# Attention on one Trainium2 core: the next group's loads put ahead of the spreading of reciprocals, and divided otherwise over four gaps

## The reference

```
qkv = (h @ Wqkv.T + bqkv).reshape(B, N, num_heads, hd, 3)
energy = einsum('bhqd,bhkd->bhqk', q, k)
att = softmax(energy, axis=-1) / D ** 0.5
out = einsum('bhqk,bhkd->bhqd', att, v)
out = out.reshape(B, N, D) @ Wp.T + bp
h1 = out + hidden
y = _sln(h1, ...) + h1
```

## Time and profile before

| | |
|---|---|
| median of 3 runs | 1860.88 us (1857.96 to 1861.51) |
| the profiled execution's own time | 1862.02 us |
| its span, first to last instruction | 1859.5 us |
| PE busy | 1810.8 us (97%) |
| POOL busy | 1217.2 us (65%) |
| DVE, ACT busy | 1256.5 us (68%), 835.2 us (45%) |
| attention | from about 900 us to 1769 us of the span |

### The profile page before, as it was taken

How to read it: one execution, slowest core, us unless ns; L and a number is a source line. 1 busy time by engine, 2 the same in 40 slices (tenths; PEclk the granted TensorE clock), 3 DMA queues, 4 the chain that set the end, 5 groups by cost and what they waited for, 6 DMA issues and landing times. The chain is left out here.

```text
span 1859.5 us, 26833 instructions
## 1 busy us (share of the span) xinstructions
PE 1810.8 (97%) x9510; PEld 1210.0 (65%) x9510; DVE 1256.5 (68%) x1986; ACT 835.2 (45%) x1545; POOL 1217.2 (65%) x679
## 2 busy tenths in 40 slices
PE   8899999999999999999999999999999999999997
PEld 4588888888888788888545554555555455544476
DVE  4665655655655565556777777787777777777487
ACT  3223122222223222221466666666666666666465
POOL 2675465465464243332588888888888898889665
PEclk9999999999999999999999999999999999999899
DMA  7310110110103667594877877787778777765796
GB/s 268 121 35 23 57 35 23 56 34 23 58 1 124 204 213 239 180 295 179 198 155 178 187 174 179 175 187 176 179 180 182 179 180 176 183 152 126 224 385 252
DMA packets 135382, 287.21 MB, mean 154 GB/s; under 512 B 23985, under 2 KB 41521, under 8 KB 127201
## 3 DMA queue, kind: packets, MB, share of 16 engines
q1 hardware_dynamic: 102996, 200.10, 35.5%
q0 software_dynamic: 9264, 66.11, 17.5%
q10 hardware_dynamic: 23008, 19.54, 3.3%
HBM read 134.68 MB, written 84.19 MB: 118 GB/s over the span
## 5 line engine op out<-in xcount | busy, mean ns | idle before, releaser
L1634 DVE TENSOR_REDUCE at_mrow<-banks 128x1 f32<-128x512 f32 x976 | 593.6, 680 | 166.0 <-PE banks L1480 165.8
L1730 POOL TENSOR_TENSOR at_sums<-at_probs 128x2048 f32<-128x2048 f32 x127 | 598.5, 4713 | 92.3 <-DMA at_sums<-at_sums 81.4
L1614 ACT ACTIVATE at_probs<-banks 128x512 f32<-128x512 f32 x1024 | 519.2, 623 | 182.1 <-PE banks L1498 176.7
L1480 PE MATMUL banks<-early_ks,early_qs 96*128 96x512 f32 x976 | 406.9, 417 | 8.8 <-DVE at_mrow L1634 5.0
L1498 PE MATMUL banks<-early_qs,early_ks 98*128 98x512 f32 x1024 | 408.9, 418 | 1.9 <-ACT at_probs L1614 1.9
L1480 PEld LDWEIGHTS banks<-early_ks,early_qs 96*128 96x128 f32 x976 | 184.8, 189 | 141.5 <-DVE at_mrow L1634 88.4
L1498 PEld LDWEIGHTS banks<-early_qs,early_ks 98*128 98x128 f32 x1024 | 193.6, 190 | 106.4 <-ACT at_probs L1614 82.5
L1510 PE MATMUL banks<-at_probs,at_v 128*32 128x512 f32 x2048 | 251.1, 608 | 0.8 <-DMA at_v<-v_scratch 0.8
L66 PE MATMUL banks<-l_nt,l_weights 128*128 128x512 f32 x768 | 177.9, 392 | 5.9 <-DVEq L1208 4.8
L662 ACT ACTIVATE l_gt<-banks,mod 128x512 f32<-128x512 f32 x60 | 45.1, 777 | 299.0 <-PE banks L528 261.4
L66 PE MATMUL banks<-l_ht,l_weights 128*128 128x512 f32 x768 | 177.4, 390 | 1.9 <-issue 1.9
(11 more groups left out here) (147 smaller groups left out, 2160.6 us busy)
## 6 DMA issues: line engine op xcount, KB each, us to landing
at_sums<-at_sums POOLq DMA_DIRECT2D x63, 1024.0 KB, 8.1
qk_scratch<-qk_out SPq DMA_DIRECT2D x64, 512.0 KB, 6.3
early_ks<-qk_scratch SPq DMA_DIRECT2D x48, 512.0 KB, 4.9
early_qs<-qk_scratch SPq DMA_DIRECT2D x96, 256.0 KB, 5.7
attn_scratch<-at_out SPq DMA_DIRECT2D x32, 512.0 KB, 7.5
o_a<-attn_scratch SPq DMA_DIRECT2D x32, 512.0 KB, 13.1
chunk_in<-x SPq DMA_DIRECT2D x8, 1024.0 KB, 5.3
v_scratch<-qk_v ACTq DMA_DIRECT2D x32, 256.0 KB, 2.6
```

Of the source, the lines that this page charges most:

```text
L1480: pe.matmul(em[n % 3][:], qs[0:96, slot, half, j, c * P:(c + 1) * P], ks[0:96, slot, j, keys * CH:(keys + 1) * CH], start=True, stop=True) ...
L1614: nc.scalar.activation(probs[:, i % 4, j, :], et[n % 3][:], ACT.Exp).then_inc(exp_done, 1)
L1634: nc.vector.tensor_reduce(mrow[:, half, keys, u:u + 1], em[n % 3][:], AX.X, ALU.max).then_inc(max_done, 1)
L1730: nc.gpsimd.tensor_tensor(into, probs[:, a], probs[:, a + 1], ALU.add).then_inc(pair_ready, 1)
```

## The change

Three things change in what SP does in attention; no other engine's order changes.

First, `load_part` divides the ten pieces otherwise: in units of 256 KB the four gaps had 5, 2, 5 and 2 and now have 3, 4, 3 and 4. By pieces they were 3, 1, 5, 1 and are 2, 3, 2, 3. Second, `widen_rden` is cut in two: `keep_rden` stores the reciprocals, `widen_rden` waits for that and loads them back. Third, gap 1 and gap 3 now stand between the two halves, so their loads are issued ahead of the loads of reciprocals. In the last group the second and the fourth gap of `load_projection` move in the same way.

```diff
-                    load_stack_keys(sp, sh, ks, g, slot, (0, 1))
+                    load_stack_keys(sp, sh, ks, g, slot, (0,))
                     load_stack_queries(sp, sh, qs, g, slot, 0, (0,))
                 if part == 1:
+                    load_stack_keys(sp, sh, ks, g, slot, (1,))
+                    load_stack_queries(sp, sh, qs, g, slot, 0, (1, 2))
+                if part == 2:
                     load_stack_keys(sp, sh, ks, g, slot, (2,))
-                if part == 2:
-                    load_stack_queries(sp, sh, qs, g, slot, 0, (1, 2))
-                    load_stack_queries(sp, sh, qs, g, slot, 1)
+                    load_stack_queries(sp, sh, qs, g, slot, 1, (0,))
                 if part == 3:
+                    load_stack_queries(sp, sh, qs, g, slot, 1, (1, 2))
                     load_v(g, slot)
...
-            def widen_rden(g, half):
+            def keep_rden(g, half):
...
                 sp.dma_start(sh.rden_d[half].rearrange("j (r c) -> (j r) c", c=DW), rden_c[:, half]).then_inc(rden_stored[half], 16)
+
+            def widen_rden(g, half):
+
+                first = isinstance(g, int) and g == 0
                 sp.wait_ge(rden_stored[half], 16 * (g + 1))
...
                 place_neg(g, slot, 1)
                 if not first:
+                    keep_rden(g - 1, 1)
+                fetch(1)
+                if not first:
                     widen_rden(g - 1, 1)
-                fetch(1)
                 fetch(2)
                 spread_den(g, 0)
...
                     place_neg(g + 1, (slot + 1) % RING, 0)
+                keep_rden(g, 0)
+                fetch(3)
                 widen_rden(g, 0)
-                fetch(3)
```

## The result

The changed kernel takes 1881.1 us (median of 6, 1876.9 to 1884.3) against 1860.2 us (median of 6, 1858.0 to 1861.5): a ratio of 1.0117, 95% interval 1.0105 to 1.0129. It is slower by 1.2%, as forecast in sign and within the range; the forecast was 1872.5, so 9 us of the 21 were missing in it. The profiled execution spans 1879.6 us, 20.1 more than that of before.

A forecast was written before the change was run, and what follows sets the result against it. POOL's chain of quad landings, adds and multiplications, not PE, was taken to set the pace. Groups +8 us and the end +3 made +11 on the profiled 1862.0: 1873, given as 1872.5 us; 8-in-10 range 1853 to 1901.

The forecast's parts named there:

- SP's DMAs are served in the order of issue: Reciprocals land behind the loads of gaps 1 and 3: 8.1 and 7.5 us after the quad.
- rival 5: Queues take turns, so quad 1 slows the loads still ahead of the reciprocals: 5.4 us more a group, 1942 us; 7%.
- `multiply` moves by 2.5 and 2.0 us: On POOL, in half 1 and half 0, the multiplication starts that much later, waiting for reciprocals behind the gap's loads.
- from `multiply` to the next quad's issue it takes 11.38 us: On POOL, the least time for this stretch; it was 12.06 us, of which 0.68 is air that the delay uses up.
- quads 0 and 2 get faster, to 7.6 us: With 512 KB less just ahead in gaps 0 and 2, landing to add included; before 9.1 and 9.5, bounds 7.2 and 8.8.
- Rival 4: Quads don't get faster (8.8 us), since their slowness is the store's doing: 1903 us; 13%.
- a group takes 53.6 us: Sum of both halves, 27.1 and 26.5 us, against 53.09 before: +0.5 us a group.
- POOL's chain: Landing, add, DMA issue, `multiply`, add, add, DMA issue, landing; said to set the halves' pace, 26.73 and 26.36 us before.
- rival 1: Emptier queue wins: reciprocals within 6.5 us, quads in 7.2, PE's own work bounds, maxima wait comes back: 1852 us; 28%.
- ACT's air of 3.4 and 3.0 us covers the delay: ACT overwrites probabilities of pairs 4 and 0 that long after POOL's adds end, barely covering delays of 2.5 and 2.0 us.
- no chain waits for quads 1 and 3: They meet a larger gap, but the second add behind `multiply` starts later than they land, so no cost.
- The end: Last group: 4.5 MB ahead of the last reciprocals; PE's last stage starts +2.4 us, 3 us in all, between 0 and 6.

The follow-up runs named there:

- the reciprocals in the middle: Changed kernel with the reciprocals of gaps 1 and 3 loaded behind the keys or v and ahead of the two loads of queries: 1855.0 us, ratio 0.9981.

## Why the prediction was right, and where its sizes were off

**That SP's DMAs are served in the order of issue** held: the reciprocals land 8.6 and 7.7 us after the quad (13 groups; forecast 8.1 and 7.5). It nearly holds across the queues too, further than the prediction used it: in the division-alone kernel POOL's quads 1, on their own queue, moved their first packet 4.3 us after the issue (1.5 us in the order-alone kernel), behind loads that SP had just issued. It isn't strict: of the 1 MB of that gap 318 KB were still to come when the packets of the quad in the rows above began, and from then on both queues moved side by side. Turn taking as rival 5 priced it (5.4 us more a group) is not what happened: the changed kernel's quads 1 took 8.1 us, and the reciprocals landed some 4.5 us before them.

**That `multiply` moves by 2.5 and 2.0 us** held: over groups 3 to 14 it starts 8.4 and 7.7 us after the landing, by 2.8 and 1.9 us later than before (5.7 and 5.8). POOL stands before it in nearly every half.

**That from `multiply` to the next quad's issue it takes 11.38 us** held (11.23 in the rows above).

**That quads 0 and 2 get faster, to 7.6 us,** held: 7.5 and 7.6. Rival 4 is out.

**That a group takes 53.6 us** is the term that was mis-sized. Over groups 3 to 14 it is 54.06 us against 53.22 before, and over all of 0 to 14 it makes +14.4 us where the sum had +8. Three traces split it. Delay: the changed kernel against the reciprocals in the middle, 813.2 - 787.1 = 26 us, 2.0 us a group; the prediction had 3.9. What is gained while nothing is late: the kernel in the middle against the kernel before, 798.7 - 787.1 = 12 us, 0.9 a group; the prediction had 3.4, all of it for the emptier gaps 0 and 2. But the order alone, with these gaps as full as before, already has 8.5 of the 12 us (790.2), because gaps 1 and 3 go out sooner, a gain that the sum didn't have; for the new division 3 us remain, which one trace can't tell from nothing. So both terms were too large, the gain by more, and the net of +0.5 us a group (measured +1.1) came as near as it did with some luck.

The sum of POOL's chain alone let a half gain what its DMAs gain, but PE's own work allows no half under about 25.85 us: with the reciprocals in the middle the halves are down to 26.2, and from 900 to 1690 us POOL stands 30.8 us for ACT before its adds, in 30 cases (8.6 us in 11 before), beside 37.5 us for the quads' DMAs (78.8 before). That PE's own work caps the gain was in rival 1 as its ceiling and should have been in the sum.

**That ACT's air of 3.4 and 3.0 us covers the delay** was argued "barely". It held: the waits of the changed kernel have none of ACT's exponentials for POOL.

**That no chain waits for quads 1 and 3** held for POOL: they land 13.2 and 12.6 us after the landing before them, and the second add behind the multiplication starts later. But PE sums these quads too, and that they could be late for it when 1 MB goes out just ahead of them is what the division alone shows; the prediction didn't price it.

**The end** was +5.1 us where 2.4 to 3 stood. The 4.5 MB and the reciprocals landed later than the 16.6 + 1.2 us assumed: the multiplication starts at 1782.67, 18.5 us after the first load's issue at 1764.20. From there to the stores it takes 3.4 us (forecast 3.55), and then PE starts 3.0 us behind the first store, not 0.8. The late start also costs clock, below.

**Rival 1** (the queue wins, 1852 us) was not this kernel but is a neighbour: with the reciprocals in the middle it is 1855.0. It named the condition rightly, reciprocals within 6.5 us. Its way to the time was another: it gave back PE's wait for the negated maxima, and that one is still 12.3 us there (12.6 before).

**What the prediction did not see** is that the two parts of the change are not additive. In the table, medians in us of the four combinations and the kernel in the middle, in brackets the ratio to the kernel before as it ran beside each:

| | old division 5, 2, 5, 2 | new division 3, 4, 3, 4 |
|---|---|---|
| reciprocals ahead of the gaps | 1859.2 (1) | 1902.7 (1.0227) |
| reciprocals behind the gaps | 1857.3 (0.9987) | 1881.1 (1.0117) |
| in the middle | no middle: one load a gap | 1855.0 (0.9981) |

The prediction priced the order as the loss and the division as the gain. Alone the division loses 43 us and the order gains 2. What is in the way is a gap of 1 MB that goes out in one piece: if late, it is just ahead of the quad, if early, it is ahead of the reciprocals. In the middle only its second half, 512 KB, goes out just ahead of the quad (on the mean 4.4 and 5.0 us after the landing, the quad at 5.5), and quads 1 land after 8.2 us instead of 10.7.

What part of the 14.4 us is TensorE's lowered clock no kernel was run to separate, but the traces bound it (next section): at most about 5 us.

## What to carry to other kernels

A small transfer that an engine waits for costs what is issued ahead of it on its queue: count the bytes between it and the landing that releases them. Here a large transfer on another queue of the same 16 DMA engines was late in the same way (quad 1 after 10.7 us). When bytes are moved to spread the load, ask of each place which small transfer follows next, and put that one in front or in the middle; here 512 KB further ahead was worth 26 us. And a chain's gain is capped by the next engine's own work, while its loss is not, so two terms of opposite sign should not be netted before the cap is applied.

## What the runs showed of the hardware

A wait of PE costs more than its length. In group 5 of the changed kernel PE stands from 1198.3 us for a quad and then for the maxima, and TensorE's granted clock falls behind it. Busy time of the engines by stretch (PE, PEld, DVE, ACT, POOL, then the granted clock, the DMA share and GB/s):

```profile
1190.00:1198.00 8.00, 8.00 (x52) 3.57 (x49) 7.39 (x15) 4.97 (x10) 7.70 (x4) 1.00 0.64 130
1198.00:1203.00 5.00, 1.37 (x20) 0.42 (x16) 0.00 (x0) 0.60 (x1) 3.25 (x2) 1.00 0.70 202
1203.00:1208.00 5.00, 4.87 (x14) 3.71 (x14) 3.68 (x6) 3.00 (x6) 2.77 (x2) 0.66 1.12 225
1208.00:1213.00 5.00, 5.00 (x29) 2.40 (x28) 3.57 (x7) 3.05 (x7) 4.56 (x2) 1.00 0.78 161
```

PE is busy for 1.37 of the 5 us from 1198, and for part of the next 5 us the clock is at the lower of its two levels (1.2 instead of 2.4 GHz; mean 0.66): 14 matmuls, against 29 in the 5 us after (not all of the same kind). That group takes 57.3 us, the longest of all. The same stands behind the longer stop at the end, in the changed kernel first and then in the kernel before:

```profile
1789.00:1793.80 4.80, 4.73 (x11) 3.79 (x12) 4.39 (x6) 3.81 (x12) 3.82 (x3) 0.50 0.84 299
```

```profile
1769.80:1774.60 4.80, 4.80 (x15) 3.88 (x16) 4.48 (x6) 3.90 (x12) 3.91 (x3) 0.68 0.78 283
```

After 7.48 us of standing PE's last stage starts with 4.8 us at 0.50, after 2.40 us at 0.68 on the mean. That agrees with the Trainium skill, "TensorE: Matmul & The Clock Gate", section "What's actually happening", which says that the engine falls to the lower clock when it idles; what it did here before each fall is in the rows.

The same rows bound what the clock costs in the groups. Behind the start of the stage, the changed kernel has these two stretches at the lower level, and the kernel before has none up to group 15:

```profile
1008.80:1015.60 6.80, 5.90 (x14) 4.65 (x15) 3.84 (x6) 3.48 (x6) 4.39 (x3) 0.50 1.00 251
1203.40:1206.80 3.40, 3.40 (x9) 2.64 (x9) 2.54 (x4) 1.84 (x4) 2.37 (x2) 0.50 1.05 206
```

```profile
905.80:1700.40 794.60, 783.08 (x4836) 403.04 (x4835) 612.40 (x1075) 520.49 (x1018) 687.09 (x264) 1.00 0.76 175
```

That is 10.2 us at half speed, so at most 5.1 us of the 14.4 (an estimate, for the profiled execution); the other 9 us and more are not the clock's.
